# A graph layer's kernel: split rows stored at once per tile, identity products in the combination, and feature products on two row groups

## The reference

```python
xn = _layernorm(x)
h = (xn @ W.T).reshape(n, 8, 32)                      # one row per node
h_src, h_dst = h[src], h[dst]                         # one row per edge
alpha = einsum('ehd,hd->eh', h_src, a_src) + einsum('ehd,hd->eh', h_dst, a_dst)
enc = relu(edge_attr @ edge_W.T + edge_b).reshape(-1, 8, 32)   # three features per edge
alpha = leaky(alpha + sum(enc * h_dst, axis=-1))
attn = softmax of alpha over the edges of one target node
out = segment_sum(h_src * attn[..., None], dst) + bias
x = x + out + mix(xn)
x = x + sum over eight experts of gate * FFN(_layernorm(x))
```

## Time and profile before

| | |
|---|---|
| median of 3 runs | 4826.66 us (4821.68 to 4843.91) |
| the profiled execution's own time | 4848.34 us |
| its span | 4846.5 us |
| TensorE busy | 4087.7 us, 84% |
| VectorE, ScalarE, GpSimd busy | 56%, 47%, 37% |
| mean granted clock of TensorE | 0.872 of 2.4 GHz |
| DMA | 629.74 MB, 130 GB/s on average |

### The profile page before, as it was taken

How to read it: one execution, slowest core, us unless ns; L and a number is a source line. 1 busy time by engine, 2 the same in 40 slices (tenths; PEclk the granted TensorE clock), 3 DMA queues, 4 the chain that set the end, 5 groups by cost and what they waited for, 6 DMA issues and landing times. The chain is left out here.

```text
span 4846.5 us, 80424 instructions
## 1 busy us (share of the span) xinstructions
PE 4087.7 (84%) x22764; PEld 1897.1 (39%) x22765; DVE 2700.2 (56%) x5470; ACT 2291.3 (47%) x6074; POOL 1780.1 (37%) x1859
## 2 busy tenths in 40 slices
PE   5699988957888887788887878878887999999999
PEld 3333322312333333333333333333333666666666
DVE  7566723336666666676666666667666333333333
ACT  4444445524555555555555555555554433333332
POOL 3255555644454445444444444445440000000000
PEclk8799989976888888888888887888887799999999
DMA  7555556655555555555555555555552100000000
GB/s 216 160 165 162 164 177 201 210 156 154 161 168 165 158 165 164 162 168 168 159 162 152 163 157 161 162 159 168 164 162 67 61 8 1 8 8 8 8 8 8
DMA packets 378173, 629.74 MB, mean 130 GB/s; under 512 B 83912, under 2 KB 245063, under 8 KB 377536
## 3 DMA queue, kind: packets, MB, share of 16 engines
q1 hardware_dynamic: 277266, 356.80, 23.4%
q0 software_dynamic: 93408, 257.23, 19.5%
q10 hardware_dynamic: 7104, 11.01, 0.7%
HBM read 520.59 MB, written 104.12 MB: 129 GB/s over the span
## 5 line engine op out<-in xcount | busy, mean ns | idle before, releaser
L1629 POOL DMA_INDIRECT s_rows<-scratch_src_rows,s_idx_w x1312 | 1257.6, 959 | 1367.6 <-PE s_ps_a L1692 563.3
L1837 DVE SCALAR_TENSOR_TENSOR s_enc<-s_enc,s_a_dst,s_ps_d 128x512 f32<-128x512 f32 x904 | 634.9, 741 | 313.3 <-DMA p_feats<-in_edge_f,p_tcol_i 160.8
L1734 ACT ACTIVATE s_enc<-s_ps_f 128x1024 f32<-128x1024 f32 x452 | 459.5, 1017 | 516.6 <-remote 265.5
L1692 PE MATMUL s_ps_a<-s_rows,s_hot_e 128*64 128x264 f32 x3616 | 647.1, 490 | 44.9 <-DVE s_rows L1920 32.4
L2285 DVE SCALAR_TENSOR_TENSOR kx_y_all<-e_ps_o,kx_gate,kx_y_all 128x256 f32 (+1 forms) x392 | 173.5, 480 | 684.2 <-PE e_ps_o L2340 684.2
L1920 DVE TENSOR_TENSOR s_rows<-s_rows,s_ps_x 128x1024 f32<-128x1024 f32 x452 | 545.7, 1207 | 13.6 <-ACT s_a_w L1765 8.7
L1688 PE MATMUL s_ps_a<-ke_sums,k_ident 128*128 x790 | 341.0, 520 | 217.1 <-DVE ke_sums L1913 123.6
L1913 DVE TENSOR_TENSOR ke_sums<-s_ps_a,ke_sums 128x264 f32 x509 | 218.3, 429 | 505.3 <-remote 263.9
L1669 PE MATMUL s_ps_s<-s_enc,s_head_sum 128*32 128x256 f32 x3616 | 353.7, 469 | 152.9 <-DVE s_enc L1837 121.2
L1779 ACT ACTIVATE s_hot_e<-k_iota_row,s_rel_w 128x64 f32<-128x64 f32 x1808 | 480.5, 339 | 0.0
L1787 ACT COPY ke_sums<-s_ps_a 128x264 f32 x395 | 148.6, 376 | 552.5 <-remote 337.8
(11 more groups left out here) (280 smaller groups left out, 5259.0 us busy)
## 6 DMA issues: line engine op xcount, KB each, us to landing
s_table<-scratch_dst_parts SPq DMA_DIRECT2D x904, 96.0 KB
s_rows<-scratch_pre_rows SPq DMA_DIRECT2D x124, 528.0 KB
s_relb<-scratch_rel_rows SPq DMA_DIRECT2D x226, 256.0 KB
scratch_pre_rows<-n_rows SPq DMA_DIRECT2D x62, 528.0 KB
scratch_pre_rows<-m_rows SPq DMA_DIRECT2D x62, 528.0 KB
s_rows<-scratch_src_rows,s_idx_w POOLq DMA_INDIRECT x1312
s_feat<-scratch_step_parts SPq DMA_DIRECT2D x226, 54.0 KB
s_pen_w<-scratch_pen_rows SPq DMA_DIRECT2D x228, 48.1 KB
```

Of the source, the lines that this page charges most:

```text
L1629: pool.indirect_dma_start(out=rows[:, d % R, m, :], out_offset=None, in_=scr["src_table"], in_offset=bass.IndirectOffsetOnAxis(ap=idx_w[:, ...
L1692: last = PE.matmul(ps_a[t * WN:(t + 1) * WN, sub, 0:SRC_W], hot_e[:, d % 3, 2 * sub + t, :], rows[:, d % R, 2 * sub + t, :], start=(sub == ...
L1734: A.activation(enc[:, d % 2], ps_f[:], ACT.Relu).then_inc(enc_made, 1)
L1837: V.scalar_tensor_tensor(out=enc[:, d % 2, c, :], in0=enc[:, d % 2, c, :], scalar=a_dst[:, c:c + 1], in1=ps_d[:, c, :], op0=ALU.add, op1=A ...
```

## The change

Four things change.

1. The split rows are stored with one transfer per tile. For that `dst_parts` is laid out as (half tile, node, part, 384), so that a partition's two parts are one piece of 1,536 bytes. The semaphore counts 16 per tile instead of 32. The table load of the edge stage reads the new layout with its source arranged as part, node, values.
2. The features stand twice, on partitions 0 to 29 and 32 to 61, each with a transfer of its own, and so do the weights; the two products of `encode` use one copy each.
3. stage_combine gets products of the identity with a part of the running sums into a bank of their own that nothing reads: four of 512 columns ahead of the first tile and one of 256 columns in each turn.
4. In the same stage TensorE waits for the router's weights at turn 19 and not at the start.

```diff
-                        for b in range(2):
-                            sp.dma_start(scr["dst_parts"][2 * d + b].rearrange("c n w -> n c w"), parts[b * WN:(b + 1) * WN, d % RP]).then_inc(d_stored[d % RP], 16)
+                        sp.dma_start(scr["dst_parts"][2 * d:2 * d + 2].rearrange("b n c w -> (b n) (c w)"), parts[:, d % RP].rearrange("p c w -> p (c w)")).then_inc(d_stored[d % RP], 16)
...
-                    wait(act, d_stored[u], 32 * (i // RP))
+                    wait(act, d_stored[u], 16 * (i // RP))
...
-        feat = s.sb("feat", [FR, RP, 2, ED], BF16)
+        feat = s.sb("feat", [32 + FR, RP, 2, ED], BF16)
...
+                sp.dma_start(w_rows[32:32 + FR, :], w_rows[0:FR, :]).then_inc(c_in, 16)
...
-                    sp.dma_start(feat[3:FR, u].rearrange("f a e -> f (a e)"), scr["step_parts"][g].unsqueeze(0).to_broadcast([3, EP, 4 * GE])).then_inc(feat_in[u], 16)
+                    for c in range(2):
+                        sp.dma_start(feat[32 * c + 3:32 * c + FR, u].rearrange("f a e -> f (a e)"), scr["step_parts"][g].unsqueeze(0).to_broadcast([3, EP, 4 * GE])).then_inc(feat_in[u], 16)
...
-                        sp.dma_start(table[:, u, sub, :], row(scr["dst_parts"], j).rearrange("o c n w -> (o c n) w")).then_inc(table_in[u], 16)
+                        sp.dma_start(table[:, u, sub, :], row(scr["dst_parts"], j).rearrange("o n c w -> c (o n) w")).then_inc(table_in[u], 16)
...
-                    pe.wait_ge(feat_in[d // 2 % RP], 16 * (d // 2 // RP + 1))
+                    pe.wait_ge(feat_in[d // 2 % RP], 32 * (d // 2 // RP + 1))
...
-                        last = PE.matmul(ps_f[:, c, :], w_rows[:, c * P:(c + 1) * P], feat[:, d // 2 % RP, d % 2, :], start=True, stop=True)
+                        last = PE.matmul(ps_f[:, c, :], w_rows[32 * c:32 * c + FR, c * P:(c + 1) * P], feat[32 * c:32 * c + FR, d // 2 % RP, d % 2, :], start=True, stop=True)
...
-                V.memset(feat[0:3], 1.0).then_inc(cleared, 1)
+                for c in range(2):
+                    V.memset(feat[32 * c:32 * c + 3], 1.0).then_inc(cleared, 1)
...
+        ps_w = s.ps("ps_w", [P, 512])
...
+                def keep_busy(columns):
+                    PE.matmul(ps_w[:, 0:columns], keep["ident"][:], keep["spare"][:, 0:columns], start=True, stop=True)
+
+                for _ in range(4):
+                    keep_busy(2 * C)
                 pe.wait_ge(band_in, 16)
-                pe.wait_ge(w_in, 32)
                 for i in range(NT + LATE + 2):
+                    if i == LATE:
+                        pe.wait_ge(w_in, 32)
+                    keep_busy(C)
                     if i < NT:
...
-        src_rows=dram("src_rows", (NT, P, SRC_W)), dst_parts=dram("dst_parts", (NJ, 2, WN, HALF), BF16),
+        src_rows=dram("src_rows", (NT, P, SRC_W)), dst_parts=dram("dst_parts", (NJ, WN, 2, HALF), BF16),
```

More of the change, by code:

```diff
@@ L373, in _ @@
                 for u in range(RP):
-                    sp.wait_ge(d_stored[u], 32 * len(range(u, NT, RP)))
+                    sp.wait_ge(d_stored[u], 16 * len(range(u, NT, RP)))
                 sp.wait_ge(qkv_in, 16)
@@ L1634, in _ @@
                 pe.wait_ge(set_up, 1)
-                pe.wait_ge(c_in, 16 * 6)
+                pe.wait_ge(c_in, 16 * 7)
                 def encode(d):
-                    pe.wait_ge(feat_in[d // 2 % RP], 16 * (d // 2 // RP + 1))
+                    pe.wait_ge(feat_in[d // 2 % RP], 32 * (d // 2 // RP + 1))
                     wait(pe, enc_made, d)
                     for c in range(2):
-                        last = PE.matmul(ps_f[:, c, :], w_rows[:, c * P:(c + 1) * P], feat[:, d // 2 % RP, d % 2, :], start=True, stop=True)
+                        last = PE.matmul(ps_f[:, c, :], w_rows[32 * c:32 * c + FR, c * P:(c + 1) * P], feat[32 * c:32 * c + FR, d // 2 % RP, d % 2, :], start=True, stop=True)
                     last.then_inc(enc_done, 1)
@@ L1816, in _ @@
                 V.tensor_scalar(high[:], keep["iota_p"][:], float(WN), float(WN), ALU.is_ge, ALU.mult).then_inc(cleared, 1)
-                dve.wait_ge(cleared, 2)
+                dve.wait_ge(cleared, 3)
                 V.tensor_tensor(p64[:], keep["iota_p"][:], high[:], ALU.subtract).then_inc(set_up, 1)
-                dve.wait_ge(c_in, 16 * 6)
+                dve.wait_ge(c_in, 16 * 7)
                 dve.wait_ge(set_up, 1)
@@ L1934, in _ @@
                     if tau == LAG:
-                        dve.wait_ge(cleared, 2 + LAG)
+                        dve.wait_ge(cleared, 3 + LAG)
                     chain = k if 0 < w <= NW else KW
@@ L2368, in build @@
         kit = Kit(nc, whole, "k_")
-        keep = dict(ident=kit.sb("ident", [P, P]), w_rows=kit.sb("w_rows", [3 + 3 * EP, C], BF16), iota_row=kit.sb("iota_row", [P, P]), iota_p=kit.sb("iota_p", [P, 1]))
+        keep = dict(ident=kit.sb("ident", [P, P]), w_rows=kit.sb("w_rows", [32 + 3 + 3 * EP, C], BF16), iota_row=kit.sb("iota_row", [P, P]), iota_p=kit.sb("iota_p", [P, 1]))
         with ExitStack() as part:
```

## The result

The changed kernel takes 5480.9 us (median of 4 runs, 5466.99 to 5484.77), against 4835.3 us for the kernel before (4 runs beside it): 1.131 times before, 95% interval 1.128 to 1.135. The forecast was about 5,530 us on 4826.7, a ratio of 1.146, with a range of 5,060 to 5,950. The result is slower, as forecast, and 49 us under the forecast.

A forecast was written before the change was run, and what follows sets the result against it. Before, a ring of TensorE, ScalarE and VectorE bounds the edge step; after, two full DMA engines. 730 - 20 - 6 + 1 = +705 us on 4,848.3 gives 5,553, about 5,530 with the median 21.7 lower; range 5,060 to 5,950.

The forecast's parts named there:

- the feature load's 3.75 us: Edge stage's opening: issue to TensorE's release for 54 KB, against 3.5 us for relb's 256 KB; read as few engines.
- 4.5 + 2.15 + 0.75 = 7.4 us per step: Edge step on the two engines: tables, other traffic, two feature copies; 7.4 us (6.65 to 8.7) against 5.785, +730 us.
- the rest: Edge step: other traffic staying on all sixteen engines, taken as 2.15 us per step.
- the busy share (2.6 us): Edge step: other traffic by DMA busy time, 3.24 us less 0.65 for the tables' part.
- the lower end, 1.9 us: Edge step: other traffic at the best rate, 46 KB per engine.
- Start and combination: Start: one store per tile, -20 us (5 to 38 gained). Combination: moved wait and identity products, -6 us (-16 to +20).
- The feature pair: Edge stage: both feature products start together, saving 0.21 or 0.43 us per step; 0 under full DMA engines.
- The 45 us: Edge stage: the feature products' gain while the step stays as it is, within 0 to 125 us.
- the ring: Edge step before the change: TensorE, ScalarE and VectorE wait on one another, no single engine full; 5.785 us per step.
- The wide load, 4,762 us: Rival, edge stage: table loads stay on sixteen engines, so the kernel is faster, 4,762 us; chance 0.11.
- The rival with gains eaten by SyncE's issues: Rival: sixteen engines, SyncE's added 181 + 244 us use up its waits; no change, about 4,825 us; chance 0.04.
- The rival of the falling clock: Rival, edge stage: sixteen engines, TensorE idles more, granted clock falls from 0.81 to 0.76; about 4,870 us; chance 0.03.

The follow-up runs named there:

- the third set: Set of runs with the feature pair alone, the combination's part alone and the start's second store on ScalarE's queue; the kernel before took 4837.9 us.
- the kernel with the old bytes: Kernel before with only the table load's source written as 2 blocks of 64 rows, every byte at its old address: 4004.8 us beside 4003.4.
- the first set: First set of experiments, in which the kernel before took 4003.4 us.

## Why the prediction was right

**The table load on two engines: shown.** The forecast read the feature load's 3.75 us as few engines, and took the new table load, with an outermost dimension of 2, to be carried by two. After, 28 fewer 4-byte packets per step and mostly two pieces under way say so; the step is the same 7.1 to 7.2 us whether SyncE has the register reads to do or not; and the same layout read as one block costs nothing. The conclusion was right, but its evidence was thin, and that it held owes something to luck. The feature load is 27 pieces of 84 ns, 0.76 us on three engines and 0.17 on sixteen: few engines account for 0.6 us of the 3.75 us, and relb, on sixteen, needed 3.5 us. The packets of the trace of before would have told it. One point of the reasoning was also too simple: the outermost dimension as written isn't what counts. Two blocks that lie behind one another in memory stay wide.

**Its price.** Forecast 4.5 + 2.15 + 0.75 = 7.4 us per step, measured 7.19. The tables' share was 4.80 us (256 pieces, 9.59 us in sum, on two engines), 0.3 above; the two feature copies 0.76, as forecast. For the rest 7.19 - 4.80 - 0.76 = 1.6 us are left against 2.15, if the two engines never rest: the term that was mis-sized. It had been drawn towards the busy share (2.6 us), in which the waiting of packets for one another counts as busy: after, all other packets come to 2.45 us per engine and step, which with 4.80 and 0.76 is more than the step. Even the lower end, 1.9 us, was above what is left. So two errors, 0.3 too little and 0.5 too much, partly cancel. The excess over the whole stage was 632 us instead of 730, and all else together came to +4 us instead of -25, which brought the total to within 49 us.

**Start and combination.** Forecast -20 us, measured -23.0; ScalarE's wait for the stores is 30.6 us instead of 50.7. The store on ScalarE's queue puts 14.5 us of it down to the load on SyncE's queue. The combination was forecast at -6 us and showed +7.7 in the profile after, but no change in the runs that test it; an identity product in a turn costs 0.6 us at the upper clock, not the 0.43 of the forecast. Two things were not in the sum at all: the first tables arrive 6 us later at the stage's opening (of the 9.7 us), and the node stages took 9.6 us longer, which is within what they differ by between the kernels of one set (the mixing stage alone 411 to 418 us in the third set).

**The feature pair.** In the sum at 0, beneath full DMA engines, and that held. The 45 us that it was to bring while the step stays as it is were wrong: alone it brings nothing (1.001). The reason is the one that the first part of the prediction gives for the ring: TensorE waited a fifth of the time, and nearly all of its 114 us of work saved became more waiting. The saving of work itself came as forecast (125 us).

**The signs.** The step (7.2), the mean DMA share (0.44), ScalarE's wait and the feature pair's length (0.41 us in the middle) came as forecast, and the table load's issue has the length that the forecast weighed (636 ns, against 0.61 us). Two signs didn't. TensorE's idle time before the table product has no releaser named s_table in the profile, but stands under "issue" (414.5 us), and as much stands before the feature product, whose loads queue on the same engines. And SyncE wasn't seen waiting for table slots; it was held inside its issues.

**The rivals.** The wide load, 4,762 us, is what the changed kernel would have been with a contiguous read: 4792.7 us beside 4853.3, which is 4,766 on the forecast's base of 4826.7. The rival with gains eaten by SyncE's issues isn't the changed kernel's case; the kernel with two transfers per table comes closest to it, and goes beyond it (1.216 times before). The rival of the falling clock isn't needed: the granted clock did fall, from 0.81 to 0.73 in the stage, but where the two engines bound the step a slower TensorE doesn't show.

No kernel here that computes the layer beats the one before by more than its measurement can tell. The one with a contiguous read is 1.2% below it, in one run each, and leaves the rows in another order.

## What to carry to other kernels

When the source of a transfer is reordered, ask whether its two slowest dimensions still lie behind one another in memory; where they don't, the number of the outermost one may be the number of engines that carry it, and the mean DMA share falls while the transfer becomes the bound. Cost such a load as bytes over those few engines, with the other traffic of the same engines on top, and compare it with the time of one step: in this kernel a sum below it cost 0.2 us, one above it all of the excess. In a trace, count the small packets that end each load; they give the number of engines before anything is changed. And before a transfer is split to make it wide again, count the issues on its queue; here the split moved the bound from two engines to SyncE.

## What the runs showed of the hardware

- Here a queue whose transfers go to full engines held the engine that issues: the issue of relb, which the change leaves alone, went from 0.43 us to 1.96 in the middle, and that of a table load to 1,110 ns when SyncE had nothing else to do. In the profile that looks like a busy SyncE with hardly a wait. The form of a load also has its own price: 0.34 us for a contiguous table, 0.63 for a narrow one where the engines aren't full.
- The number of engines of a load can be counted in a trace: 4-byte packets come to 16 for each wide load, 2 for a narrow table load and 3 for a feature load.
- The page "DMA: Bandwidth & Descriptors" of the Trainium skill (section "Why a DMA increments its semaphore by 16 and not by 1") gives the number of engines by the slowest dimension of both sides, as the instruction carries it. The changed load (two engines) and the feature load (three) agree with it. The source written as 2 by 64 rows that lie behind one another would not, if the rule were read on the program's text: it stayed wide, 4.24 us per step. But the instruction's record reads 128 by 1 there, as before, so the run doesn't speak against the rule.
- The kernel before ran in 4003 us in one set and in 4853 in the next on the same chip, and the granted clock doesn't explain it, though the expectation for the feature pair put it down to that. From 200 to 470 us, in the same stage, first before and then the kernel with the old bytes of the first set:

```profile
200.00:470.00 270.00, 248.19 (x1880) 88.91 (x1881) 188.50 (x260) 118.75 (x491) 153.41 (x163) 0.97 0.51 163
```

```profile
200.00:470.00 270.00, 269.40 (x2655) 111.32 (x2655) 260.94 (x364) 164.32 (x681) 203.56 (x215) 0.99 0.71 217
```

  The clock is 0.97 and 0.99, and yet 2,655 products are done in place of 1,880. In the trace of before 12% of SyncE's register moves of 29 ns take over 300 ns; in the four traces of the first set none does. What pauses the engines in the one case is open. It matters for what a change is worth: the layout alone cost 28% in the set where the ring was fast, and its step of 6.80 us was no better for it.
